# A four-stage expert pipeline, four buffers for normed rows, and logits read ahead of the maxima

## The chip, the cores and the metric

One core of one Trainium2 chip runs the whole kernel in one launch. The metric is the device time in microseconds, the median of several runs; before the change it is 1592.26 us.

## What is computed

Input: 16 sequences of 256 tokens with 256 features, float32. Two layers; in each, the attention part and the expert part both read the same normed rows, and both are added to the residual:

```
xn = layernorm(x)
x  = x + mamba(xn) + moe(xn; 8 experts, top 2, inner 512) + shared_ffn(xn; inner 512)
xn = layernorm(x)
x  = x + causal_attention(xn; 16 heads of 16) + moe(xn; 8 experts, top 2, inner 128) + shared_ffn(xn; inner 256)
```

The router takes a softmax over 8 logits per token, keeps the two largest and divides them by their sum. An expert computes silu(x Wg) * (x Wu) Wd.

## The kernel before

Sequences are the unit of the dense stages, tiles of 128 tokens of one expert the unit of the expert stages. Every engine has its own instruction list, all loops around the change are unrolled in Python, and the order in which a list holds the stages of different sequences or tiles is written out by hand; engines meet only at semaphores (`wait` and `mark` of an `Event`; the `credit` of an event is how far its producer may run ahead of its consumer).

The stages in order of time:

1. **Front of layer 0**, 0 to about 227 us (`first_turns`, line 130). For each of 16 sequences VectorE computes mean and variance, GpSimd the inverse root (L648), VectorE the normed rows (`norm_apply`, L1036, writing `XN`, L1042), SyncE stores them to `xn_rows` (L554), TensorE transposes them (L1600), ScalarE copies the transposes out (L812, L814), TensorE computes logits, VectorE reads them, picks two experts and computes each token's place in its expert's list, and GpSimd scatters token numbers into the lists (L657). The shared feed-forward runs between these on TensorE, ScalarE and VectorE. `XN` has two buffers. SyncE's queue also carries the loads of `x`, of the expert weights (8 loads of 1 MB into `WGU`, L556) and behind the last store those of `ARENA` (L558).
2. **Experts of layer 0**, 227 to 622 us, 71 tiles (`tile_turns`, L145; `experts` on three engines). GpSimd gathers a tile's rows (`gather_tile`, L703, L707) into a ring of four.
3. **Mamba**, 622 to 840 us.
4. **Attention of layer 1**, 840 to 1310 us: 16 turns of about 27 us (`attention` on each engine: L963 TensorE, L972 ScalarE, L1485 VectorE, L747 GpSimd). In one turn TensorE works on sequence b's scores, on d's weighted sums, on o's projection, and for the next sequence a on transposes, logits, queries and keys. VectorE computes the maxima of each group of heads (`maxima`, L1453) and shifts the queries by them (`shift`, L1461). PSUM bank 4 holds a's transposes, then its logits and rank sums, then its queries; so `queries(a, 0)` (L1877) waits until VectorE has copied the logits (`lgc`, L1057) and, for every second a, has read the rank sums (`rkc`, L1102).
5. **Experts of layer 1**, 1310 to 1514 us, 2 x 39 tiles (`last_turns`, L150), small: eight matmul records for gate and up together, two for the transpose, two for down. Eight of the 16 sequences of the shared feed-forward (`UPS`, L37; `EARLY`, L38) are laid between tile turns, and from tile 47 on (`FINALS_AT`) GpSimd issues one gather of the final sum (`fetch_final`, L767, L772) behind each tile's gather.
6. **The end**, 1514 to 1593 us: the other eight sequences of the feed-forward, the second half of the final gathers (which wait until the last tile is stored), the final sums on VectorE (`finish`, L1549) and the stores.

A turn of an expert stage, per engine, with tile j its middle stage:

```
TensorE   gate(j)  [up(j)]  xt(j+1)  down(j-1)
ScalarE   silu(j)  xt_copy(j+1)  y_copy(j-1)
VectorE   weights(j+1)  h(j)
```

`gate(j)` (L1799) needs `xt_copy(j)` (L903), which waits for the two transposes of `xt(j)` (L1793) of the turn before.

In VectorE's attention turn the order was: `maxima(b,2,0)`, `shift(b,0)`, `maxima(b,2,1)`, then `logits_stage(a)` and `place_tokens` (L1094: rank sums, then eleven small operations that make slots). TensorE's order is: rank sums, logits of a, `scores(1, now(2), now(0))`, `queries(a,0)`, `keys(a,0)`, `scores(0, now(3), now(0))`.

Of the kernel before, what the change touches and what calls it, by code (L numbers as in the profile page):

```python
# [18 lines left out]
P = 128  # L19
NSEQ, SEQ, D = 16, 256, 256  # L20
# [15 lines left out]
N1 = 2 * NH  # L36
UPS = {20: 0, 40: 1, 46: 2, 52: 3, 58: 4, 64: 5, 70: 6, 76: 7}  # L37
EARLY = len(UPS)  # L38
# [106 lines left out]
def tile_turns(count):  # L145

    return [[tile(t - k, count) for k in range(3)] for t in range(count + 2)]


def last_turns():  # L150


    end = N1 + 2
    for t in range(end + NSEQ - EARLY + 2):
        up = UPS.get(t) if t < end else EARLY + t - end
        down = UPS.get(t - 1) if t < end else EARLY + t - end - 1 if t > end else None
        last = (t - FINALS_AT - 3) // 4 if t < end and (t - FINALS_AT - 3) % 4 == 0 else EARLY + t - end - 2 if t > end + 1 else None
        yield t, [tile(t - k) for k in range(3)], *(None if n is None else of(n) for n in (up, down, last))

# [18 lines left out]
def program(nc, ctx, a, out):  # L178
# [82 lines left out]

    XN = [sb(f"XN{u}", [P, CH, D]) for u in range(2)]
    xT = [sb(f"xT{u}", [P, KD, SEQ]) for u in range(2)]
    stats = sb("stats", [P, CH, 6])
# [114 lines left out]
    def norm_events(l):  # L379
        b = l * NSEQ  # L380
        n = {name: ev(f"norm_{name}", credit, 1, eng, b) for name, credit, eng in (
            ("var", 0, None), ("rstd", 0, None), ("xn", 0, None), ("tr", 2, "tensor"), ("xT", 2, "scalar"),
            ("lg", 2, "tensor"), ("lgc", 2, "vector"))}
        n["stored"] = [ev(f"norm_stored{u}", 1, 16, "sync", b // 2) for u in range(2)]
        n["chain"] = Chain(norm_chain, 2, b)
        return n
# [135 lines left out]
    def _(eng):  # L522
# [27 lines left out]
        for n in range(NSEQ):  # L550
            if n + 6 < NSEQ:
                load_x(n + 6)
            N[0]["xn"].wait(eng, n)
            N[0]["stored"][n % 2].mark(eng.dma_start(rows0[:, n * CH:(n + 1) * CH, :], XN[n % 2][:, :, :]))  # L554
            if 3 <= n < 3 + E:
                eng.dma_start(wgu0[:, n - 3, :, :], a["gu0"][n - 3].rearrange("(k p) n -> p k n", p=P)).then_inc(s_wgu0, 16)  # L556
        for e in range(E):
            eng.dma_start(wdn0[:, e, :, :], a["dn0"][e].rearrange("(c p) n -> p c n", p=P)).then_inc(s_wdn0, 16)  # L558

# [48 lines left out]
    def _(eng):  # L608
# [101 lines left out]
        eng.wait_ge(s_slots, 1)  # L710
        for u in range(2):
            N[0]["stored"][u].wait(eng, NSEQ // 2 - 1)
        for j in range(NJ):
# [89 lines left out]
    def _(eng):  # L803
# [94 lines left out]
        def experts(l):  # L898
            x = EX[l]

            def xt_copy(r):
                x["xt"].wait(eng, r.n)
                x["xtc"].mark(act(XGT[r.u], bank[4][:, 0:KD * P].rearrange("p (k t) -> p k t", k=KD), ACT.Copy))  # L903

            def silu(r):
                x["g"].wait(eng, r.n)
                x["h"].wait(eng, r.n, 1)
                w = I0 if l == 0 else I1
                x["sg"].mark(act(SE[:, 0:w], bank[r.u][:, 0:w], ACT.Silu))  # L909

            def y_copy(r):
                x["dn"].wait(eng, r.n)
                x["out"][r.v].wait(eng, r.i, 1)
                x["yo"].mark(act(YO[r.v], bank[6 + r.u][:, 0:D], ACT.Copy))

            def body(new, r, old):
                if r:
                    silu(r)
                if new:
                    xt_copy(new)  # L920
                if old:
                    y_copy(old)
            return body
# [94 lines left out]
    def _(eng):  # L1018
# [17 lines left out]
        def norm_apply(l, r):  # L1036
            ne = N[l]
            ne["rstd"].wait(eng, r.n)
            ne["stored"][r.u].wait(eng, r.half, 1)
            ne["tr"].wait(eng, r.n, 2)  # L1040
            for c in range(CH):
                ins = ts(XN[r.u][:, c, :], X[:, bass.ds(r.n * CH + c, 1), :].rearrange("p a d -> p (a d)"),  # L1042
                         mv[r.u][:, c, 0:1], rstd[r.u][:, c:c + 1], ALU.subtract, ALU.mult)
            ne["xn"].mark(ins)
            ne["xn"].wait(eng, r.n)
# [47 lines left out]

        def place_tokens(l, m):  # L1094

            RT[l]["rank"].wait(eng, m)
            tiles = bass.ds(m * TB, TB)
            ranks = route_bank[l][:, RANK_AT:RANK_AT + (TB + 1) * E].rearrange("p (t e) -> p t e", e=E)
            ch = RT[l]["schain"]
            ch.start(eng, m)  # L1100
            ch(tt(at, ranks[:, 0:TB, :], run_e.unsqueeze(1).broadcast_to([P, TB, E]), ALU.add))
            RT[l]["rkc"].mark(tt(run_e, run_e, ranks[:, TB, :], ALU.add))  # L1102
            tt(pick[:, 0, :, :], at, OH[0][:, tiles, :], ALU.mult)
            ch(tt(pick[:, 1, :, :], at, OH[1][:, tiles, :], ALU.mult))
# [8 lines left out]
            ch.end()  # L1113
            RT[l]["slot"].mark(tt(slot_l[:, :, tiles], line, tile, ALU.bitwise_or))

        table_count = [0]
# [108 lines left out]
        def experts(l):  # L1225
# [32 lines left out]

            def body(new, r, old):
                if new and l == 1:  # L1260
                    both_weights(new)
                if new and l == 0 and new.n:
                    gate_weights(new)
                if r:
                    h_stage(r)
                if new and l == 0 and new.n:
                    up_weights(new)

# [216 lines left out]
        def attention(c, a, b, d, o):  # L1485
# [22 lines left out]
            if b:  # L1508
                maxima(b, 2, 0)
                shift(b, 0)  # L1510
                maxima(b, 2, 1)
            if a:
                logits_stage(1, a)
                if a.v == 0 and not is_first(a):
                    place_tokens(1, a.i - 1)
                if a.n == NSEQ // 2:
                    table_index(1)
                    next_lists()
                if a.n == 13:
                    list_done(1)  # L1520
                if a.v == 1:
                    pick_experts(1, a.i, [0])
# [63 lines left out]
    def _(eng):  # L1586
# [6 lines left out]
        def norm_stage(l, r):  # L1593
            ne = N[l]
            ne["xn"].wait(eng, r.n)
            ne["xT"].wait(eng, r.n, 1)
            b = bank[5 if l == 0 else 4]
            for c in range(CH):
                for k in range(KD):
                    ins = eng.transpose(b[:, k * SEQ + c * P:k * SEQ + (c + 1) * P],  # L1600
                                        XN[r.u][:, c, k * P:(k + 1) * P], ident[:, :])
            ne["tr"].mark(ins)
# [183 lines left out]
        def experts(l):  # L1786
# [38 lines left out]

            def body(new, r, old):
                if r:
                    gate(r)
                    if l == 0:
                        up(r)  # L1830
                if new:
                    xt(new)
                if old:
                    down(old)
            return body
# [241 lines left out]
```

## Time and profile before

| | |
|---|---|
| median of 3 runs | 1592.26 us (1591.78 to 1592.51) |
| profiled execution | 1595.26 us, its span 1593.5 us |
| mean granted TensorE clock | 0.954 |
| busy, share of the span | PE 91%, weight load 72%, VectorE 53%, ScalarE 33%, GpSimd 36% |
| matmul records | 10753 |
| moved by DMA | 94.77 MB, mean 59 GB/s |

Start times in rows are microseconds from the span's start. PE is TensorE, PEld its weight loads, DVE VectorE, ACT ScalarE, POOL GpSimd. L1591 is the helper through which nearly all matmuls are issued, so groups are told apart by their tiles: `score` is banks 0 to 3, `side` banks 4 and 5, `mixed` banks 6 and 7. The profile names an allocation and not a view of it: `ARENA`, `WGU`, `sh_gu` and `w_in` stand for whatever lies in them at the time (`WGU<-score` L1458 are the maxima).

### The profile page before, as it was taken

What the parts mean: (1) busy time and instruction counts of PE and PEld (TensorE: products, weight loads), DVE (VectorE), ACT (ScalarE), POOL (GpSimd) and SP (SyncE); (2) the same over time, 40 slices, a digit from 0 to 9 for tenths busy, and PEclk for the clock granted to TensorE, in tenths of its full rate; (3) what the DMA queues carried; (4) which work ended last, traced back from release to release, by engine and by line L of the source; (5) the groups of instructions that cost most, each with busy time, mean ns of one, the idle gap of its engine ahead of it and who ended that gap; (6) DMA issues with size and microseconds to landing.
All of it is one profiled execution on the core that took longest, in us unless ns stands there. A gap on an engine that the chain in (4) does not pass through costs nothing.

```text
span 1593.5 us, 29535 instructions
## 1 busy us (share of the span) xinstructions
PE 1453.8 (91%) x10753; PEld 1151.7 (72%) x10753; DVE 839.1 (53%) x2307; ACT 526.5 (33%) x1099; POOL 578.4 (36%) x762
## 2 busy tenths in 40 slices
PE   7996999999999998999997899999998979997866
PEld 6886789999999997666665566666665647776744
DVE  4554444444444443788875666666666534333414
ACT  2221122222222222333332545454444434433300
POOL 2444421111111111222224455646563454455460
PEclk9998999999999999999997999999999989999987
DMA  5893811111111114100002111111100004434431
GB/s 177 149 104 44 99 48 50 52 47 48 48 50 51 47 48 122 38 0 0 0 0 64 31 31 32 28 34 27 36 21 15 2 18 129 134 119 133 120 123 62
DMA packets 73185, 94.77 MB, mean 59 GB/s; under 512 B 14877, under 2 KB 61367, under 8 KB 73056
## 3 DMA queue, kind: packets, MB, share of 16 engines
q1 hardware_dynamic: 55440, 56.54, 15.6%
q0 software_dynamic: 17616, 36.48, 8.3%
q8 instruction: 84, 1.38, 0.4%
q14 instruction: 45, 0.37, 0.1%
HBM read 60.66 MB, written 32.31 MB: 58 GB/s over the span
## 4 chain that ended last, share of the span: by engine, by line
PE 86%; DVE 5%; issue 4%; DMA 2%; ACT 1%; another core or an unknown queue 1%; POOL 0%; DVEq 0%; ACTq 0%; POOLq 0%
PE score L1591 49%; PE mixed L1591 18%; PE side L1591 13%; DVE WGU L1458 2%; PE side L1793 2%; DMA xn_rows<-XN 2%; PE side L1600 1%; PE mixed L1960 1%; PE side L1953 1%; PE side L1739 0%; PE side L1858 0%; DVE stats L1027 0%; DVE X L1483 0%; DVE X L1558 0%
## 5 line engine op out<-in xcount | busy, mean ns | idle before, releaser
L707 POOL DMA_INDIRECT XN<-xn_rows,slot_tok x149 | 141.4, 949 | 399.5 <-PE side L1793 365.3
L1458 DVE TENSOR_REDUCE WGU<-score 128x2 f32<-128x256 f32 (+1 forms) x256 | 130.8, 553 | 153.3 <-PE score L1591 151.2
L1591 PE MATMUL score<-xT,HT 128*128 128x128 f32 x1136 | 208.0, 275 | 0.0
L743 POOL TENSOR_SCALAR_AFFINE_SELECT ARENA<-ARENA 128x256 f32<-128x256 f32 x256 | 104.2, 431 | 185.1 <-ACT ARENA L944 184.0
L1591 PEld LDWEIGHTS score<-xT,HT 128*128 128x128 f32 x1136 | 166.8, 192 | 0.0
L944 ACT ACTIVATE ARENA<-score 128x768 f32<-128x768 f32 x128 | 103.8, 811 | 148.3 <-PE score L1591 145.9
L1257 DVE TENSOR_TENSOR HT<-sh_gu,score 128x128 f32<-128x128 f32 (+1 forms) x149 | 71.3, 478 | 148.7 <-ACT sh_gu L909 71.3
L657 POOL DMA_INDIRECT lists<-token_no,w_in x128 | 125.4, 980 | 44.2 <-issue 32.3
L1591 PE MATMUL score<-ARENA 32*128 32x256 f32 (+1 forms) x2048 | 126.8, 353 | 12.0 <-DVE WGU L1458 6.0
L1591 PE MATMUL mixed<-ARENA,HT 128*128 x568 | 134.2, 379 | 0.0
L909 ACT ACTIVATE sh_gu<-score 128x128 f32<-128x128 f32 (+1 forms) x149 | 64.1, 430 | 191.3 <-PE score L1591 172.8
L1591 PE MATMUL score<-XT,sh_gu 128*128 128x256 f32 x512 | 120.3, 395 | 2.7 <-issue 2.7
L1232 DVE COPY xT<-WGU 128x256 f32 x142 | 35.5, 291 | 156.7 <-PE score L1591 155.9
L1591 PEld LDWEIGHTS score<-XT,sh_gu 128*128 128x128 f32 x512 | 101.2, 200 | 17.7 <-issue 3.3
L1591 PE MATMUL score<-xT 128*128 128x128 f32 x568 | 109.8, 275 | 2.4 <-issue 2.0
L1591 PEld LDWEIGHTS mixed<-ARENA,HT 128*128 128x128 f32 x568 | 102.5, 190 | 11.0
L1591 PEld LDWEIGHTS score<-xT,WGU 128*128 128x128 f32 x624 | 77.3, 193 | 45.6 <-ACT xT L903 35.2
L1591 PE MATMUL score<-xT,sh_gu 128*128 128x128 f32 x568 | 109.8, 275 | 0.0
L1591 PEld LDWEIGHTS score<-ARENA 32*128 32x128 f32 x2048 | 73.2, 188 | 50.3 <-issue 45.0
L1591 PE MATMUL side<-xT,WGU 128*128 128x256 f32 x256 | 88.6, 496 | 21.4 <-DVE w_in L1102 11.1
L1591 PE MATMUL score<-xT,WGU 128*128 128x128 f32 x624 | 89.7, 287 | 20.0 <-ACT xT L903 13.8
L1202 DVE TENSOR_TENSOR HT<-SG,score 128x256 f32<-128x256 f32 x96 | 39.7, 419 | 113.2 <-ACT SG L822 88.2
(249 smaller groups left out, 2714.8 us busy)
## 6 DMA issues: line engine op xcount, KB each, us to landing
y_rows<-sh_gu SPq DMA_DIRECT2D x149, 128.0 KB
xn_rows<-XN SPq DMA_DIRECT2D x32, 256.0 KB
WGU<-in_gu SPq DMA_DIRECT2D x8, 1024.0 KB
X<-in_u SPq DMA_DIRECT2D x16, 256.0 KB
ARENA<-in_dn SPq DMA_DIRECT2D x8, 512.0 KB
out<-X SPq DMA_DIRECT2D x16, 256.0 KB
XN<-xn_rows,slot_tok POOLq DMA_INDIRECT x149
lists<-token_no,w_in POOLq DMA_INDIRECT x128
```

The costliest lines, as they stand in the source:

```text
L657: eng.indirect_dma_start(lists, bass.IndirectOffsetOnAxis(slot_l[:, k, t:t + 1], 0), tok_i[:, t:t + 1], None).then_inc(s_scat[g], 16)
L707: x["got"][j % RING].mark(eng.indirect_dma_start(XG[j % RING], None, xn_rows[l], bass.IndirectOffsetOnAxis(slot_tok[:, j:j + 1], 0)))
L743: ins = eng.affine_select(out=m, in_=m, compare_op=ALU.is_ge, fill=0.0, base=0, pattern=[[0, 2], [1, P]], channel_multiplier=-1)
L909: x["sg"].mark(act(SE[:, 0:w], bank[r.u][:, 0:w], ACT.Silu))
L944: A["exp"][h].mark(act(PT[i % 2][:, 2 * h:2 * h + 2, :, :].rearrange("p r b q -> p r (b q)"), score[:, 2 * h:2 * h + 2, 0:HALVES * P], ACT ...
L1202: f["ht"].mark(tt(inner_rows(l, r, i), SG[i % 2][:, :], inner(l, r, i)[:, SEQ:2 * SEQ], ALU.mult))
L1232: ins = eng.tensor_copy(to, wgu0[:, bass.ds(expert(r), 1), k, first * P:end * P].rearrange("p a (c n) -> p (a c) n", n=P))
L1257: x["h"].mark(tt(HET[r.u][:, 0:w // P, :], parts(SE[:, 0:w]), parts(up), ALU.mult))
L1458: ins = eng.tensor_reduce(o, score[:, 2 * h:2 * h + 2, c * P:(2 * c + 1) * P], AX.X, ALU.max, negate=True)
L1591: return eng.matmul(o, l, r, start=start, stop=stop)
L1600: ins = eng.transpose(b[:, k * SEQ + c * P:k * SEQ + (c + 1) * P], XN[r.u][:, c, k * P:(k + 1) * P], ident[:, :])
L1793: ins = eng.transpose(bank[4][:, k * P:(k + 1) * P], XG[r.v][:, k * P:(k + 1) * P], ident[:, :])
```

## The change

The edits:

- **Expert turns have four stages**, in both layers: `xt` and `xt_copy` work on tile j+2 while gate works on j, and on TensorE `down` goes ahead of `xt`, on ScalarE `y_copy` ahead of `xt_copy`. VectorE's weights stay one tile ahead of gate. Each stage has one more turn.
- **Seven sequences of the feed-forward** instead of eight are laid between the tiles of layer 1, from the third on seven turns apart instead of six; nine are left for the end. The final sums move by two turns.
- **Four buffers for `XN` in the front of layer 0**: the two new ones lie in the part of `ARENA` that the last expert's down weights fill later; SyncE waits before that one load until both are stored and transposed.
- **VectorE's attention turn**: `logits_stage` and the rank sums stand between `shift(b,0)` and `maxima(b,2,1)`; the slots are made behind it. The copy of the turned list (a = 13) moves along with the logits.

```diff
-UPS = {20: 0, 40: 1, 46: 2, 52: 3, 58: 4, 64: 5, 70: 6, 76: 7}
+UPS = {20: 0, 40: 1, 46: 2, 53: 3, 60: 4, 67: 5, 74: 6}
...
-    return [[tile(t - k, count) for k in range(3)] for t in range(count + 2)]
+    return [[tile(t - k, count) for k in range(4)] for t in range(count + 3)]
...
-    end = N1 + 2
+    end = N1 + 3
+    finals = {FINALS_AT + 5 + 4 * n: n for n in range(EARLY)}
...
-        last = (t - FINALS_AT - 3) // 4 if t < end and (t - FINALS_AT - 3) % 4 == 0 else EARLY + t - end - 2 if t > end + 1 else None
-        yield t, [tile(t - k) for k in range(3)], *(None if n is None else of(n) for n in (up, down, last))
+        last = finals.get(t) if t < end else EARLY + t - end - 2 if t > end + 1 else None
+        yield t, [tile(t - k) for k in range(4)], *(None if n is None else of(n) for n in (up, down, last))
...
+    last_dn = ARENA[:, (E - 1) * I0 // P * D:].rearrange("p (u c d) -> p u c d", u=2, c=CH)
+    XN0 = [t[:, :, :] for t in XN] + [last_dn[:, u, :, :] for u in range(2)]
...
         for e in range(E):
+            if e == E - 1:
+                N[0]["tr"].wait(eng, NSEQ - 1)
+                for v in (2, 3):
+                    N[0]["stored"][v].wait(eng, NSEQ // len(XN0) - 1)
...
-            def body(new, r, old):
+            def body(new, ahead, r, old):
                 if r:
                     silu(r)
+                if old:
+                    y_copy(old)
                 if new:
                     xt_copy(new)
-                if old:
-                    y_copy(old)
...
             ne["rstd"].wait(eng, r.n)
-            ne["stored"][r.u].wait(eng, r.half, 1)
+            if l == 0:
+                rows, turn = XN0[r.n % len(XN0)], r.n // len(XN0)
+                ne["stored"][r.n % len(XN0)].wait(eng, turn, 1)
+            else:
+                rows = XN[r.u]
+                ne["stored"][r.u].wait(eng, r.half, 1)
...
                 shift(b, 0)
-                maxima(b, 2, 1)
             if a:
                 logits_stage(1, a)
                 if a.v == 0 and not is_first(a):
-                    place_tokens(1, a.i - 1)
+                    rank_sums(1, a.i - 1)
+                if a.n == 13:
+                    list_done(1)
+            if b:
+                maxima(b, 2, 1)
+            if a:
+                if a.v == 0 and not is_first(a):
+                    place_slots(1, a.i - 1)
                 if a.n == NSEQ // 2:
                     table_index(1)
                     next_lists()
-                if a.n == 13:
-                    list_done(1)
...
                 if r:
                     gate(r)
                     if l == 0:
                         up(r)
+                if old:
+                    down(old)
                 if new:
                     xt(new)
-                if old:
-                    down(old)
```

The hunks behind the list of `XN0` are, in this order, of SyncE's queue, ScalarE's expert turn, `norm_apply`, VectorE's attention turn and TensorE's expert turn. `rank_sums` and `place_slots` are the two halves of the old `place_tokens`, operation for operation.

## Rows read from the trace of the kernel before

**Rows 1.** The page, part 4: engines' shares of the chain that ended last
```profile
PE 86%; DVE 5%; issue 4%; DMA 2%; ACT 1%; another core or an unknown queue 1%; POOL 0%; DVEq 0%; ACTq 0%; POOLq 0%
```

**Rows 2.** Busy time by stretch: us of each engine, clock, DMA, GB/s
```profile
1400.00:1500.00 100.00, 84.55 (x504) 70.94 (x503) 37.35 (x102) 33.00 (x104) 59.40 (x63) 0.97 0.44 134
...
1540.00:1594.00 54.00, 27.97 (x98) 21.40 (x98) 21.86 (x49) 3.72 (x10) 13.49 (x15) 0.69 0.24 76
```

**Rows 3.** PE's timeline, 119 to 140 us (start, us, instruction, idle before)
```profile
122.19 0.66 PE L1600 MATMUL side<-ident,XN 128*128 128x128 f32 x4 [0.86 <-issue]
...
138.07 1.12 PE L1600 MATMUL side<-ident,XN 128*128 128x128 f32 x4 [10.98 <-DVE XN L1042]
```

**Rows 4.** VectorE's and GpSimd's timelines of the same stretch
```profile
121.39 0.74 DVE L1042 TENSOR_SCALAR XN<-X,mv,rstd 128x256 f32<-128x256 f32 x2 [3.23 <-issue]
...
137.28 0.74 DVE L1042 TENSOR_SCALAR XN<-X,mv,rstd 128x256 f32<-128x256 f32 x2 [9.00 <-DMA xn_rows<-XN]
...
128.37 0.72 POOL L648 TENSOR_TENSOR rstd<-rstd,minus_half 128x2 f32<-128x2 f32 x1 [4.71 <-DVE rstd L1034]
```

**Rows 5.** The waits, 860 to 1290 us (total us, times, longest)
```profile
PE side L1591 <- DVE w_in L1102: 11.1, 7, 1.6
...
PE side L1591 <- DVE LG L1057: 8.6, 7, 1.3
```

**Rows 6.** The chain that ended last, 860 to 1290 us (start, us, what)
```profile
872.36 3.78 PE side L1591 x8
...
898.91 1.97 PE side L1591 x8
...
1053.36 1.73 PE side L1591 x8
```

**Rows 7.** Busy time about one such wait, columns as in Rows 2
```profile
1006.00:1009.00 3.00, 1.99 (x5) 1.66 (x6) 2.45 (x14) 0.18 (x1) 1.73 (x3) 0.61 0.12 33
```

**Rows 8.** VectorE's timeline, 1055 to 1067 us, and a row of PE's
```profile
1057.36 0.86 DVE L1466 SCALAR_TENSOR_TENSOR ARENA<-side,head_mask,ARENA 128x256 f32<-128x256 f32 x2
1060.15 1.02 DVE L1458 TENSOR_REDUCE WGU<-score 128x2 f32<-128x256 f32 x2 [1.93 <-PE score L1591]
...
1066.04 0.17 DVE L1128 COPY w_in<-w_in 128x8 f32<-128x8 f32 x1
...
1057.88 1.04 PE L1591 MATMUL side<-WGU,xT 128*128 128x8 f32 x8
```

**Rows 9.** The waits, 1300 to 1520 us, and the chain, 1363 to 1399 us
```profile
PEld score L1591 <- ACT xT L903: 35.2, 50, 3.1
...
1363.66 1.16 PE score L1591 x8
...
1365.51 1.16 PE score L1591 x8
...
1391.43 4.34 PE score L1591 x24
...
1396.43 2.62 PE score L1591 x16
```

**Rows 10.** Costliest groups, 1402 to 1516 us (times, busy us, mean ns, idle before)
```profile
L772 POOL DMA_INDIRECT ARENA<-y_rows,slot x32 | 30.7, 959 | 9.7 <-issue 9.7
L707 POOL DMA_INDIRECT XN<-xn_rows,slot_tok x31 | 29.9, 964 | 31.2 <-PE side L1793 15.2 <-remote 10.8 <-issue 5.2
```

**Rows 11.** GpSimd's timeline at the end
```profile
1517.82 0.94 POOL L772 DMA_INDIRECT ARENA<-y_rows,slot  x1 [15.86 <-DMA y_rows<-sh_gu]
...
1556.81 0.95 POOL L772 DMA_INDIRECT ARENA<-y_rows,slot  x1 [0.30 <-issue]
```

**Rows 12.** The chain, 1515 to 1564 us
```profile
1528.51 3.45 PE score L1591 x16
...
1534.95 0.38 PE score L1591
...
1562.37 0.77 PE score L1591
```

More of the change, by code:

```diff
@@ L383, in norm_events @@
             ("lg", 2, "tensor"), ("lgc", 2, "vector"))}
-        n["stored"] = [ev(f"norm_stored{u}", 1, 16, "sync", b // 2) for u in range(2)]
+        n["stored"] = [ev(f"norm_stored{u}", 1, 16, "sync", b // len(XN0)) for u in range(len(XN0) if l == 0 else 2)]
         n["chain"] = Chain(norm_chain, 2, b)
@@ L553, in _ @@
             N[0]["xn"].wait(eng, n)
-            N[0]["stored"][n % 2].mark(eng.dma_start(rows0[:, n * CH:(n + 1) * CH, :], XN[n % 2][:, :, :]))
+            v = n % len(XN0)
+            N[0]["stored"][v].mark(eng.dma_start(rows0[:, n * CH:(n + 1) * CH, :], XN0[v]))
             if 3 <= n < 3 + E:
@@ L710, in _ @@
         eng.wait_ge(s_slots, 1)
-        for u in range(2):
-            N[0]["stored"][u].wait(eng, NSEQ // 2 - 1)
+        for v in range(len(XN0)):
+            N[0]["stored"][v].wait(eng, NSEQ // len(XN0) - 1)
         for j in range(NJ):
@@ L1038, in norm_apply @@
             ne["rstd"].wait(eng, r.n)
-            ne["stored"][r.u].wait(eng, r.half, 1)
+            if l == 0:
[4 more added lines that the diff above has]
+                ne["stored"][r.u].wait(eng, r.half, 1)
             ne["tr"].wait(eng, r.n, 2)
             for c in range(CH):
-                ins = ts(XN[r.u][:, c, :], X[:, bass.ds(r.n * CH + c, 1), :].rearrange("p a d -> p (a d)"),
+                ins = ts(rows[:, c, :], X[:, bass.ds(r.n * CH + c, 1), :].rearrange("p a d -> p (a d)"),
                          mv[r.u][:, c, 0:1], rstd[r.u][:, c:c + 1], ALU.subtract, ALU.mult)
@@ L1092, in pick_experts, with rank_sums @@
             RT[l]["hot"].mark(tt(hot_b[:, tiles, :], OH[0][:, tiles, :], OH[1][:, tiles, :], ALU.add))
-        def place_tokens(l, m):
+        def rank_sums(l, m):
             RT[l]["rank"].wait(eng, m)
-            tiles = bass.ds(m * TB, TB)
             ranks = route_bank[l][:, RANK_AT:RANK_AT + (TB + 1) * E].rearrange("p (t e) -> p t e", e=E)
@@ L1102, in place_tokens, with place_slots @@
             RT[l]["rkc"].mark(tt(run_e, run_e, ranks[:, TB, :], ALU.add))
+        def place_slots(l, m):
+            tiles = bass.ds(m * TB, TB)
+            ch = RT[l]["schain"]
             tt(pick[:, 0, :, :], at, OH[0][:, tiles, :], ALU.mult)
@@ L1114, in place_tokens @@
             RT[l]["slot"].mark(tt(slot_l[:, :, tiles], line, tile, ALU.bitwise_or))
+        def place_tokens(l, m):
+            rank_sums(l, m)
+            place_slots(l, m)
         table_count = [0]
@@ L1257, in h_stage, with body @@
                 x["h"].mark(tt(HET[r.u][:, 0:w // P, :], parts(SE[:, 0:w]), parts(up), ALU.mult))
[L1259 to L1263, printed above, removed]
+            def body(new, ahead, r, old):
+                if ahead and l == 1:
+                    both_weights(ahead)
+                if ahead and l == 0 and ahead.n:
+                    gate_weights(ahead)
                 if r:
                     h_stage(r)
-                if new and l == 0 and new.n:
-                    up_weights(new)
+                if ahead and l == 0 and ahead.n:
+                    up_weights(ahead)
             def first():
@@ L1597, in norm_stage @@
             b = bank[5 if l == 0 else 4]
+            rows = XN0[r.n % len(XN0)] if l == 0 else XN[r.u]
             for c in range(CH):
@@ L1600, in norm_stage @@
                     ins = eng.transpose(b[:, k * SEQ + c * P:k * SEQ + (c + 1) * P],
-                                        XN[r.u][:, c, k * P:(k + 1) * P], ident[:, :])
+                                        rows[:, c, k * P:(k + 1) * P], ident[:, :])
             ne["tr"].mark(ins)
@@ L1824, in down, with body @@
                 x["dn"].mark(ins)
-            def body(new, r, old):
+            def body(new, ahead, r, old):
                 if r:
```

## The prediction

> **What bounds the kernel now.** I read the chain that ended last first, then busy time by stretch, then the waits of each stretch, and only at disputed places the timelines. TensorE holds 86% of the chain [rows 1]; what it waits for, or does slowly, is the time to be had. A stretch where it is always busy gives nothing, so I looked for stretches where it is not: 84.55 of 100 us in the late tiles of layer 1, 27.97 of 54 us at the end at a granted clock of 0.69 [rows 2]. The experts of layer 0 are packed, and there I expect nothing but about +0.5 us for the extra turns.
>
> **1. Four buffers for normed rows.** The transposes at 138.07 waited 10.98 us for the normed rows [rows 3]; VectorE had begun them at 137.28 after 9.00 us of waiting for a store to leave `XN` [rows 4]. What is late next is the inverse root: it ends at 128.37+0.72=129.09, so with a free buffer the rows (0.74 us) are there at 129.83 and the transposes start near 130.0 instead of 138.07, 8.1 us sooner. The wait of 0.86 us at 122.19 [rows 3] belongs to the same pair of buffers (VectorE's rows began at 121.39 [rows 4]). Sum **-8.9**. The store that a buffer needs next is four sequences back, over 20 us earlier, and 9 us were the most that one was late. SyncE's queue gets one new wait, ahead of the last down weights only; behind it stand loads for experts 100 us later, so I cost it at nothing; uncovered it would be one late load of that kind, up to 9 us. Bounds -6 (a later sequence takes 3 us back) and -11.
>
> **2. Logits ahead of the maxima.** Between 860 and 1290 us TensorE waits 11.1 us for the rank sums and 8.6 us for the logits' copy, 7 times each [rows 5]. VectorE starts the second half's maxima only when the scores end, idle 1.93 us before; the logits (1.04 us from 1057.88) end at 1058.92 and the shift (0.86 from 1057.36) at 1058.22 [rows 8]. So copy and sums, some 0.5 us, fit into that idle time, before 1060.15, and both waits go: **-19.7**. Maxima, if late, have cover: TensorE comes to their buffer behind queries and keys, 1.73 us at full clock, against 1.02 for the maxima [rows 8], 0.7 us. Its bounds are -15 (0.35 us a turn left) and -19.7.
>
> **3. The clock behind those waits.** Queries and keys are eight records: 3.78 us at 872.36, 1.97 at 898.91 [rows 6]. Of the 15 such rows of the turns 13 take 3.43 to 3.78 us, 3.57 on average, which is half speed (1.2 of 2.4 GHz); about one of the waits the granted clock is 0.61 [rows 7]. Eight records of another stage, with work ahead of them, take 1.73 at 1053.36 [rows 6], 0.216 each. A wait stands in front of every slow row but the first, at 872.36, so I let the clock go with the wait: twelve turns from 3.57 to 1.97, and in the fourteen turns with waits 0.24 us from 1.97 to 1.73: 19.2+3.4=**-22.6**. Bounds 0 and -22.6. One rule speaks against this. The Trainium skill, "TensorE: Matmul & The Clock Gate", Part 4 on PE-mode transpose, says that transposes don't count as activity the way matmuls do. Attention has transposes in every turn, which the change leaves there; by that rule the clock would stay low without any wait, and this term would be nothing.
>
> In the turn a=8 the table is now built ahead of the other maxima of the next group: it holds VectorE to 1066.04 [rows 8], where these are due 3 us behind the last. 2.4 us of wait and 1.7 us of slow records: **+4.1**, bounds 0 and +5.
>
> **4. Tile turns of layer 1.** One turn is 1365.51-1363.66=1.85 us [rows 9], four parts in a chain: gate 1.16, transposes, down, and a wait for ScalarE's copy: 35.2 us over 50 waits of the weight load on `xT` [rows 9]. Gate costs 1.16 because its first load waits; where eight feed-forward records stand ahead of it the sixteen take 2.62 [rows 9], of which 8 x 0.216=1.73 (the side records, [rows 6]) are theirs, and gate has 0.89. Transposes and down take 1396.43-(1391.43+4.34)=0.66. With the copy a whole turn old, a turn is 0.89+0.66=1.55, 0.31 less. About 40 turns stand before the final gathers start: **-12**. The nearest floor is GpSimd's issue: 0.96 us busy [rows 10], and in the final burst (1556.81-1517.82)/31=1.26 from one to the next [rows 11], under 1.55. Bounds 0 and -15.
>
> **5. The late tiles.** From 1402 to 1516 us GpSimd issues 32 final gathers and 31 tile gathers, 30.7 and 29.9 us busy; before the latter it is idle 31.2 us, put down to TensorE's transposes and to an unknown releaser [rows 10]. TensorE is idle there too [rows 2], so neither is plainly the bound. One feed-forward sequence leaves this stretch (its 5.18 us comes back in 6), but GpSimd's two issues per tile, 2.5 us, may then hold the tiles. Between the two I take **-4**: nearest to the row that says GpSimd still waits for TensorE for 15.2 us. Bounds +10 (GpSimd holds all tiles) and -20 (idle time of TensorE gone).
>
> **6. The end.** Nine sequences stand behind the tiles, not eight: 3.45+1.73 us [rows 12, 6], **+5.2**. But from 1534.12 to 1562.37 the chain has a record only every (1562.37-1534.95)/13=2.1 us [rows 12], while GpSimd issues final gathers back to back from 1517.82 to 1557.8 [rows 11]: TensorE seems held by that burst. The sequence more is dearer if it falls into it. Bounds +5.2 and +30.
>
> **Sum:** 0.5-8.9-19.7-22.6+4.1-12-4+5.2=-57.4. The profiled execution has 1595.26 us (span 1593.5) and would come to 1537.9; the median of the runs, 1592.26, is 3.0 lower: **1535**.
>
> **The rivals.** A measurement of this kernel can tell about 0.2% (3.2 us) from no change.
>
> - *The tile turns give nothing* (0.14): the ring of four fills at GpSimd's pace, since gathers are issued when `XG` is freed by a transpose, and terms 4 and 5 fall away, +16. For it: GpSimd's idle time is partly "issue" [rows 10]. Against: PE's load waits for ScalarE, 35.2 us, not for a gather. **1551**.
> - *The clock stays low in attention* (0.09): something else in the turn than the wait lowers it. For: the two turns at 1.97 don't show why they are spared. Against: the rows of a turn that have work ahead of them are at full clock [rows 6]. Term 3 gives nothing, +22.6: **1558**. That is what the page's rule on transposes would make of it; the front speaks against it, where four transposes take 0.66 us behind a wait of 0.86 and 1.12 behind one of 10.98 [rows 3], so that they follow the wait.
> - *The tail's held stretch goes* (0.08): with TensorE further behind or ahead of the burst, the 13 records between 1534.95 and 1562.37 take 0.216 instead of 2.1 us each, 13 x 1.9=-24: **1511**.
> - *VectorE is late in the shorter attention turns* (0.05): with turns some 3 us shorter the eleven slot operations and maxima compete, 0.7 us in each of 14 turns: +10, **1545**.
> - *Slower: TensorE is held while GpSimd issues back to back* (0.04). The mechanism of the tail, in two places: with the copy a turn early GpSimd no longer waits for transposes in the late tiles [rows 10] and issues back to back there too. Each record so held costs 2.1-0.2=1.9 us. The whole extra sequence of the tail (24 records) and as many in the late tiles are 48 x 1.9=91: 1535+91=**1626**. It decides from 57/1.9=30 held records on. Against: the late tiles have fewer records beside the burst after the change, and GpSimd's waits there have TensorE as releaser.
> - *No effect* (0.02): the waits come back under other names, as when VectorE's order is right but each turn is set by ScalarE: **1592**.
>
> The forecast has 0.58.
>
> **How the numbers follow.** 1535 is the likeliest case. Its own bounds lie in terms 3 to 6; 1508 holds the case of the freed tail and nearly all of -20 in term 5, 1562 holds the cases at 1545, 1551 and 1558 with what can go wrong in one of them besides. What is left out is the slower rival, no effect, and mixtures of two large misses. Within 0.2%: 0.02, from "no effect"; slower: 0.04, from the last mechanism; faster: the rest, 0.94.
>
> **What would show each step.** (1) TensorE's wait at 127 to 138 us shrinks from 10.98 to about 3; the wait for `xn_rows` leaves VectorE's list. (2) Both groups of waits of [rows 5] vanish, the attention turn falls by (19.7+22.6)/14=3.0 us. (3) All rows of queries and keys stand at 1.73 to 1.97 us; at 3.5 with the waits gone, the clock rival is right. The turn a=8 alone shows a wait for `WGU`. (4) The weight load's wait for `xT` is gone and early turns are 1.55 us apart; at 1.85, the first rival holds, and what TensorE waits for (`XT`, an unknown releaser) says whose pace it is. (5) The stretch from the first final gather to the last tile is 4 us shorter with nine feed-forward sequences behind; GpSimd without idle time there and TensorE with more would prove me wrong. (6) Nine sequences at the end, each 5.18 us outside the burst; records 2 us apart over more than one sequence point to the slower mechanism. The forecast as a whole is wrong if attention does not end at least 35 us sooner relative to its start.

## The result, and the profile after

The changed kernel takes 1543.97 us (median of 4 runs, 1535.74 to 1551.84) beside 1592.12 us before (4 runs): a ratio of 0.9697, 95% interval 0.9633 to 0.9761, so 48 us or 3.0% less. The forecast was 1535 us with a range of 1508 to 1562: the measured time lies in the range, 9 us above the forecast. The profiled execution is the fastest of the four: 1535.74 us, its span 1533.2 us, 60.3 us shorter than the span of before. The table cuts both spans at the same instructions of GpSimd. That is the first thing to do with two traces: where a stage comes out equal, nothing was won or lost in sum (though two effects can still cancel in it).

| stretch | before | after | difference |
|---|---|---|---|
| start to the first gather of layer 0 | 221.5 | 211.6 | -9.9 |
| to the first gather of layer 1 | 1079.6 | 1036.3 | -43.3 |
| to the first early final gather (the early tiles) | 101.5 | 91.4 | -10.1 |
| to the first final gather of the burst (the late tiles) | 115.2 | 114.4 | -0.8 |
| to the last one | 39.0 | 39.0 | 0.0 |
| to the end (the rest of the span) | 36.7 | 40.5 | +3.8 |

The burst is what GpSimd does behind the last tile: it issues the last 32 final gathers one after the other.

**Front.** TensorE's timeline of the changed kernel answers [rows 3]: the wait of 10.98 us is 1.93, and the next group of transposes stands at 127.23 instead of 138.07.

```profile
127.23 0.76 PE L1626 MATMUL side<-ident,XN 128*128 128x128 f32 x4 [1.93 <-DVE XN L1055]
...
137.37 0.63 PE L1626 MATMUL side<-ident,ARENA 128*128 128x128 f32 x4
```

**Attention.** Both groups of [rows 5] are gone from TensorE's waits; the longest entries left are those for maxima and shift, which were there before with 6.0 and 4.4 us. Columns: total us, times, longest.

```profile
PE score L1616 <- DVE WGU L1479: 7.9, 8, 2.7
PE score L1616 <- DVE ARENA L1487: 4.9, 5, 1.9
```

The chain shows queries and keys at full clock, where [rows 6] had 3.78, and beside them the exception, the first turn (859.15). (Columns: start, us, what.)

```profile
859.15 2.96 PE side L1616 x8
...
1004.32 1.73 PE side L1616 x8
...
1056.63 1.73 PE side L1616 x8
```

The granted clock of the stretch about the second of them, the column before the DMA share, is 1.00 in the busy time by stretch, against 0.61 in [rows 7].

```profile
1003.00:1006.00 3.00, 3.00 (x32) 2.15 (x31) 1.66 (x6) 1.59 (x3) 1.63 (x3) 1.00 0.23 56
```

**Tiles.** In a typical early turn the chain has no wait left: from one gate to the next 1315.28-1313.73=1.55 us, against 1.85 in [rows 9].

```profile
1313.73 0.89 PE score L1616 x8
1314.62 0.43 PE mixed L1616 x2
1315.06 0.22 PE side L1819 x2
1315.28 0.89 PE score L1616 x8
```

Not every turn is like that. In three turns, of 2.2 to 2.4 us, VectorE has operations on the tables of tiles, slots and weights in front of the copy of an expert's weights (L1266), and gate starts only 0.1 us after that copy ends. One of them:

```profile
1279.97 0.48 DVE L1196 TENSOR_REDUCE route_small<-SG 128x16 f32<-128x128 f32 x2
...
1280.66 0.42 DVE L1266 COPY WGU<-WGU 128x512 f32 x1
...
1281.18 1.13 PE L1616 MATMUL score<-xT,WGU 128*128 128x128 f32 x8 [0.50 <-issue]
```

**The late tiles and the end.** The late tiles took as long as before with one feed-forward sequence less in them. GpSimd's two groups are those of [rows 10] almost number for number; what differs is its idle time ahead of the tile gathers, 27.2 us instead of 31.2, with 10.6 instead of 15.2 us put down to TensorE's transposes. The part without a known releaser ("remote") stayed, 10.5 beside 10.8.

```profile
L780 POOL DMA_INDIRECT ARENA<-y_rows,slot x32 | 31.2, 976 | 9.7 <-issue 9.7
L715 POOL DMA_INDIRECT XN<-xn_rows,slot_tok x31 | 29.8, 962 | 27.2 <-PE side L1819 10.6 <-remote 10.5 <-issue 5.5
```

In the timeline GpSimd issues transfers with 0.3 us between them. ScalarE waits 3.93 us, until 1384.28, for the gate whose eight records stand at 1379.12 to 1380.25, and TensorE starts again when GpSimd has paused:

```profile
1378.17 0.97 POOL L715 DMA_INDIRECT XN<-xn_rows,slot_tok  x1 [0.30 <-issue]
...
1379.12 1.13 PE L1616 MATMUL score<-xT,WGU 128*128 128x128 f32 x8 [0.64 <-issue]
...
1379.44 0.95 POOL L780 DMA_INDIRECT ARENA<-y_rows,slot  x1 [0.30 <-issue]
...
1380.70 0.95 POOL L715 DMA_INDIRECT XN<-xn_rows,slot_tok  x1 [0.31 <-issue]
...
1381.95 0.95 POOL L780 DMA_INDIRECT ARENA<-y_rows,slot  x1 [0.30 <-issue]
...
1384.28 0.28 ACT L917 ACTIVATE sh_gu<-score 128x128 f32<-128x128 f32 x1 [3.93 <-remote]
...
1385.03 0.69 PE L1616 MATMUL mixed<-WGU,HT 128*128 x2 [3.22 <-DVE HT L1278]
```

At the end GpSimd issues 32 final gathers from 1453.74 to 1493.6, and from 1470.8 on TensorE has one record in 0.7 to 3.5 us, with nothing to wait for ("issue"), until 1498.9. That is the held stretch of [rows 12], about as long as before.

```profile
1453.74 0.94 POOL L780 DMA_INDIRECT ARENA<-y_rows,slot  x1 [18.24 <-DMA y_rows<-sh_gu]
...
1480.67 0.58 PE L1616 MATMUL score<-XT,WGU 128*128 128x256 f32 x1 [1.52 <-issue]
...
1483.45 0.58 PE L1616 MATMUL score<-XT,WGU 128*128 128x256 f32 x1 [2.20 <-issue]
...
1492.69 0.95 POOL L780 DMA_INDIRECT ARENA<-y_rows,slot  x1 [0.30 <-issue]
...
1493.96 0.59 PE L1616 MATMUL score<-XT,WGU 128*128 128x256 f32 x1 [2.91 <-issue]
```

TensorE's own rows don't show all of it. Outside such stretches ScalarE's silu of the feed-forward starts 0.42 us after the start of the last of the eight records that it needs. In the burst the silu at 1466.56 comes 4.2 us after its record (1462.32), and the two of the group at 1464.26, with last records at 1465.78 and 1467.50, come 26.1 and 31.4 us after them. VectorE's sum at 1472.94 comes 8.5 us after the end of its eight records, which begin at 1462.54.

```profile
1462.54 1.89 PE L1616 MATMUL side<-WGU,HT 128*128 128x256 f32 x8
1464.26 3.62 PE L1616 MATMUL score<-XT,WGU 128*128 128x256 f32 x16
1466.56 0.38 ACT L830 ACTIVATE SG<-score 128x256 f32<-128x256 f32 x1 [5.17 <-PE score L1616]
...
1472.94 0.69 DVE L1228 TENSOR_TENSOR X<-X,side 128x512 f32<-128x512 f32 x1 [5.54 <-remote]
...
1491.87 0.38 ACT L830 ACTIVATE SG<-score 128x256 f32<-128x256 f32 x1 [24.93 <-remote]
...
1498.89 0.66 ACT L830 ACTIVATE SG<-score 128x256 f32<-128x256 f32 x2 [6.64 <-remote]
```

So by what the other engines get from TensorE the hold begins some 9 us into the burst (1462.3 against 1453.74), earlier than TensorE's gaps say. The ends of matmul records are modelled, so the trace doesn't tell whether TensorE finished late or the others were held as well. "TensorE is held" stands below for this whole effect.

### The profile page after: what moved, and what is told of

The parts are those of the page before. It is cut to its first block, busy times and chain, and to the rows that moved or that the text cites. A ratio compares the mean times of both kernels' runs of the same rounds, so it can differ in the third digit from the quotient of the medians.

```text
span 1533.2 us, 29539 instructions
## 1 busy us (share of the span) xinstructions
PE 1420.3 (93%) x10753; PEld 1139.0 (74%) x10753; DVE 826.0 (54%) x2307; ACT 516.3 (34%) x1099; POOL 579.7 (38%) x762
## 4 chain that ended last, share of the span: by engine, by line
PE 87%; DVE 4%; another core or an unknown queue 3%; issue 3%; ACT 1%; POOL 1%; DVEq 0%; POOLq 0%; ACTq 0%
PE score L1616 49%; PE mixed L1616 20%; PE side L1616 13%; PE side L1819 2%; PE side L1626 1%; DVE WGU L1479 1%; PE mixed L1986 1%; PE side L1979 1%; PE side L1765 1%; DVE stats L1035 0%; PE side L1884 0%; POOL lists L665 0%; DVE X L1583 0%; DVE ARENA L1390 0%
## 5 line engine op out<-in xcount | busy, mean ns | idle before, releaser
L922 ACT ACTIVATE sh_gu<-mixed 128x256 f32<-128x256 f32 x149 | 57.1, 383 | 224.6 <-PE mixed L1616 216.9
L830 ACT ACTIVATE SG<-score 128x256 f32<-128x256 f32 x96 | 36.3, 383 | 185.6 <-PE score L1616 128.8
L1616 PE MATMUL score<-xT,WGU 128*128 128x128 f32 x624 | 86.0, 282 | 5.8 <-ACT xT L911 3.6
```

The costliest lines, as they stand in the source:

```text
L830: f["sg"].mark(act(SG[i % 2][:, :], inner(l, r, i)[:, 0:SEQ], ACT.Silu))
L1616: return eng.matmul(o, l, r, start=start, stop=stop)
```

## The experiments

Each kernel was timed beside the kernel before on the same chip. Those chips differ (before had medians of 1595, 1590 and 1603 us in the three groups of runs, against 1592), and the runs of one kernel with four or more of them spread by 4 to 20 us there, so ratios count. Each cut of code shows the main lines of an edit and leaves the rest out. Group one: each edit by itself, and the changed kernel with eight sequences between the tiles.

**Four buffers alone.** Its edit, on the kernel before:

```diff
+    XN0 = [t[:, :, :] for t in XN] + [last_dn[:, u, :, :] for u in range(2)]
...
-            N[0]["stored"][n % 2].mark(eng.dma_start(rows0[:, n * CH:(n + 1) * CH, :], XN[n % 2][:, :, :]))
+            v = n % len(XN0)
+            N[0]["stored"][v].mark(eng.dma_start(rows0[:, n * CH:(n + 1) * CH, :], XN0[v]))
```

> The kernel before with the four buffers for normed rows alone. My theory: the two waits of TensorE in the front go, the first gather of layer 0 comes 9 to 10 us sooner, and nothing later takes it back: 1583 us (-9). The rival (the gain is taken back where the last down weights now wait): the first experts of layer 0 wait for weights, 1592 us.

Measured: ratio 0.9972 (0.9951 to 0.9993), 4.5 us instead of 9. The waits did go: the last transposes of the front stand at 144.96 instead of 154.50. But the first gather came at 223.0, no sooner than before's 221.5. The 9.5 us were lost again between 153 and 193 us (the feed-forward's groups start 9.5 us sooner than before at 145.5 and 4.3 us later at 193.5). Part of it went in held stretches like those at the end; TensorE's idle time put down to "issue" in the rest of the front is 8.8 us against 3.4 in the kernel before: GpSimd issues eight scatters to the lists in a row, and TensorE's records, which wait for nothing, come 2 to 3 us apart.

```profile
143.54 0.96 POOL L664 DMA_INDIRECT lists<-token_no,w_in  x1 [4.18 <-DVE w_in L1126]
...
144.96 0.66 PE L1613 MATMUL side<-ident,ARENA 128*128 128x128 f32 x4 [1.27 <-DVE ARENA L1054]
...
152.37 0.96 POOL L664 DMA_INDIRECT lists<-token_no,w_in  x1 [0.30 <-issue]
...
153.54 0.17 PE L1603 MATMUL mixed<-w_r,xT 128*128 128x12 f32 x1 [0.88 <-issue]
156.34 0.17 PE L1603 MATMUL mixed<-w_r,xT 128*128 128x12 f32 x1 [2.63 <-issue]
158.44 1.25 PE L1603 MATMUL mixed<-w_r,xT 128*128 128x12 f32 x6 [1.93 <-issue]
```

The same buffers taken out of the changed kernel:

```diff
-            v = n % len(XN0)
-            N[0]["stored"][v].mark(eng.dma_start(rows0[:, n * CH:(n + 1) * CH, :], XN0[v]))
+            N[0]["stored"][n % 2].mark(eng.dma_start(rows0[:, n * CH:(n + 1) * CH, :], XN[n % 2][:, :, :]))
```

> The changed kernel without the four buffers for normed rows, so with two. My theory of the buffers (8.9 us of waits go and nothing takes them back): 7 to 10 us slower than the changed kernel, 1549 to 1552. The rival, as the run with the buffers alone suggests (part of the gain is lost to held stretches of TensorE later in the front, or the wait covered such a stretch): 3 to 6 us slower, and the two waits of 8 to 11 us for VectorE's normed rows are back.

Measured: ratio 0.9744 (0.9705 to 0.9782) against 0.9697, some 7 us slower, with intervals that overlap. TensorE's waits for normed rows are 28.1 us in 8 waits, against 15.1 and 16.3 us in the two traces of the changed kernel, so 12 to 13 us of waits are back:

```profile
PE side L1613 <- DVE XN L1043: 28.1, 8, 7.7
```

By the two runs the buffers are worth 4.5 to 7 us in the median, not 8.9.

**VectorE's order alone.**

```diff
                 shift(b, 0)
-                maxima(b, 2, 1)
             if a:
                 logits_stage(1, a)
...
+            if b:
+                maxima(b, 2, 1)
```

> The kernel before with VectorE's new order in attention alone. My theory: both groups of waits go, 19.7 us, and the clock with them, 22.6 us, so 1592 - 42 + 4 (the turn with the table) = 1554, at most 1550. The rival (the clock is low there for another reason than the wait): only the waits go, 1572 to 1576, and queries and keys still take 3.4 to 3.8 us.

Measured: ratio 0.9766 (0.9726 to 0.9805), 37 us less, 1556 us. That is the sum with the clock in it (38 us by the prediction's terms); the waits alone would have given 1572 to 1576. In its trace queries and keys take 1.73 us in nearly every turn and 3.27 in the first. The rival in which something else lowers the clock is out. (The chain, the first turn and a later one:)

```profile
871.64 3.27 PE side L1603 x8
...
1017.04 1.73 PE side L1603 x8
```

**Four-stage turns alone.**

```diff
-    return [[tile(t - k, count) for k in range(3)] for t in range(count + 2)]
+    return [[tile(t - k, count) for k in range(4)] for t in range(count + 3)]
...
-            def body(new, r, old):
+            def body(new, ahead, r, old):
```

> The kernel before with four-stage expert turns alone, eight feed-forward sequences still between the tiles. My theory: a turn without a sequence takes 1.55 us instead of 1.85 until the final gathers start, 40 x 0.31 = 12 us, and nothing or a little more in the late tiles: 1580 (1575 to 1585). The rival (TensorE is held while GpSimd issues back to back, and it now does so sooner): part of the 12 us comes back in the late tiles, 1586 to 1600.

Measured: ratio 0.9906 (0.9873 to 0.994), 15 us less, 1579.5 us; early tiles 91.8 us instead of 101.5, late tiles 112.3 instead of 115.2. Of what the late tiles could have given, 31 times 0.3 us, only a third came.

**Eight sequences between the tiles.**

```diff
-UPS = {20: 0, 40: 1, 46: 2, 53: 3, 60: 4, 67: 5, 74: 6}
+UPS = {20: 0, 40: 1, 46: 2, 52: 3, 58: 4, 64: 5, 70: 6, 76: 7}
```

> The changed kernel with eight feed-forward sequences between the tiles, six turns apart, as before the change. Theory A (the end is set by the last tile, GpSimd's 40 us of final gathers behind it, in which TensorE does three sequences and then is held, and the sequences left after that): the last tile is 5 us later and one sequence less is left, the same within 3 us. Theory B (my sum, where the ninth sequence costs 5.2 us at the end and frees less in the late tiles): 1 to 5 us faster than the changed kernel. If more sequences collide with pairs of gathers in the late tiles: 5 to 15 us slower.

Measured: ratio 0.966 (0.9597 to 0.9724), beside 0.9697: no difference that these runs can tell; if there is one, the move to seven sequences cost a few us. In its trace the late tiles take 109.0 us with one sequence more in them than the changed kernel's 114.4, and the end behind the burst is 4.6 us shorter.

**What holds TensorE.** Six traces of group one and of before and after have the same end: the first wait of TensorE over 0.6 us comes 17 to 20 us after the burst's first gather, its first stage behind the held stretch starts 7.0 to 7.3 us after the last gather's start, whatever stood in between. So the held stretch moves with the burst. Group two gave GpSimd a pause (`pause(5)`: five fills of 128x128, each awaited, 1.3 us together; its definition isn't shown) or took the burst away.

```diff
         for q in range(NSEQ * CH, NSEQ * CH * TOPK):
+            if q % (CH * TOPK) == 0:
+                pause(5)
             fetch_final(q)
```

> The changed kernel with a pause of GpSimd of about 1.3 us ahead of every four of the 32 final gathers at the end. Theory A (TensorE is held, one instruction in 0.7 us or more, once GpSimd has issued indirect transfers back to back for some time): the held stretch at the end goes, the burst is 10 us longer, the end comes 10 to 20 us sooner. Theory B (TensorE is held by the gathers' traffic as such, or by their number): the held stretch stays and lasts as long as the burst, so the end comes 8 to 12 us later.

Measured: 1519.16 us (1510.79 to 1528.84), ratio 0.9539 (0.9467 to 0.9611), against 1541.95 us for the changed kernel on the same chip: 23 us faster, more than the 10 to 20 expected, with all 32 gathers still there. The burst is 49.8 us long instead of 39, and TensorE isn't held at all: every silu in it comes 0.42 us after its record. TensorE is busy 43.10 of 52 us there, against 23.60 of 46. Columns of the two windows, here of this kernel: length, busy us of PE, PEld, DVE, ACT, POOL, clock, DMA share, GB/s. The core's DMA moves 119 GB/s here and 99 there, so the sum of its traffic isn't what holds TensorE.

```profile
1469.00:1521.00 52.00, 43.10 (x200) 37.61 (x198) 26.24 (x58) 6.50 (x17) 38.53 (x68) 0.97 0.39 119
```

The same of the changed kernel:

```profile
1453.00:1499.00 46.00, 23.60 (x93) 17.92 (x92) 5.79 (x13) 2.40 (x7) 30.46 (x32) 0.75 0.33 99
```

The surplus is stores of results, which are late in the changed kernel. The gathers' own queue moved 4.07 MB in the 52 us and 4.20 MB in the 46, 78 and 91 GB/s: with pauses they are spread out a little, and no run tells the pauses from the lower pace of the gathers. (Columns: packets, MB, share.)

```profile
q0 software_dynamic: 1488, 4.07, 27.0%
```

```profile
q0 software_dynamic: 1536, 4.20, 30.8%
```

GpSimd's timeline with pauses shows one between two groups of four:

```profile
1469.73 0.95 POOL L790 DMA_INDIRECT ARENA<-y_rows,slot  x1 [0.50 <-POOL rest L665]
...
1473.49 0.94 POOL L790 DMA_INDIRECT ARENA<-y_rows,slot  x1 [0.30 <-issue]
1474.43 1.28 POOL L665 MEMSET rest<- 128x128 f32 x5
1476.21 0.95 POOL L790 DMA_INDIRECT ARENA<-y_rows,slot  x1 [0.51 <-POOL rest L665]
```

The chain now ends with the last gather's landing, so GpSimd is the bound there and no longer TensorE:

```profile
1519.53 2.79 DMA ARENA<-y_rows,slot
```

For comparison the changed kernel itself:

> The changed kernel once more, for comparison with the others on the same chip and for its spread: 1535 to 1552.

Measured: 1541.95 us (1540.23 to 1544.43), ratio 0.9701 (0.9636 to 0.9767).

And without the burst. This kernel leaves the last 32 final gathers out, so its results are wrong and only its time counts; the wait for them goes too.

```diff
-        for q in range(NSEQ * CH, NSEQ * CH * TOPK):
-            fetch_final(q)
```

> The changed kernel without the 32 final gathers behind the last tile (the final sums of sequences 8 to 15 then use whatever lies in the buffers). Both theories: no held stretch, TensorE does its nine sequences in 9 x 5.18 = 47 us, and the kernel ends 25 to 30 us sooner, near 1510. If a held stretch of records 1.4 to 2.1 us apart still shows there, GpSimd's issues are not its cause.

Measured: 1518.23 us (2 runs), 24 us less than the changed kernel beside it, where I had 25 to 30, and no held stretch at the end. The pauses get as much as leaving the gathers out.

**The front with pauses.**

```diff
             if a and a.n > 2:
                 if a.n == 3:
                     eng.wait_ge(s_zero, 16)
+                pause(5)
```

> The changed kernel with a pause of about 1.3 us ahead of each group of four scatters to the lists in the front of layer 0. Theory A: the held stretches there (2 to 6 us each, at a different place in every run) go, the first gather of layer 0 comes at 210 us in each run, and the spread narrows: 0 to 8 us faster than the changed kernel. Theory B: no difference, or 1 to 2 us slower where GpSimd is late.

Measured: 1537.4 us (1533.12 to 1548.86), ratio 0.9692 (0.961 to 0.9775). The spread is not narrower, and the difference to the changed kernel isn't distinguishable. In its trace one held record is left in the front, 0.78 us, against three or four in the two traces of the changed kernel; that is one trace, and it settles nothing about the time.

**The late tiles.** Group three took the early final gathers out (the results are wrong then, and only the time counts), or put pauses there:

```diff
             if j >= FINALS_AT and done < NSEQ * CH:
-                fetch_final(done)
                 done += 1
```

> The changed kernel without the 32 final gathers between the late tiles (sequences 0 to 7 then use whatever lies in the buffers). If these gathers hold TensorE, tile turns stay at 1.55 us up to the last tile and the stretch of late tiles is 92 to 95 us instead of 114, ending near 1520; if tiles are set by something else, it stays above 105 us.

Measured: ratio 0.9523 (0.9473 to 0.9573), 1528.05 us where before has 1603.17. From the 48th gather of layer 1 to the last it is 70.6 us; the changed kernel has 94.0 (1338.08 to 1432.06).

```profile
1349.73 0.94 POOL L715 DMA_INDIRECT XN<-xn_rows,slot_tok  x1 [0.61 <-DMA y_rows<-sh_gu]
...
1420.34 0.94 POOL L715 DMA_INDIRECT XN<-xn_rows,slot_tok  x1 [0.85 <-issue]
```

Between these two gathers lie 30 tile turns: 30 at 1.55 and four sequences at 5.18 are 67.2 us, and three turns with longer waits make the rest. So TensorE is nearly packed there once the final gathers are gone, and these cost 23.4 us in the changed kernel. Up to the burst, the end of the stretch, it is 90.3 us without them and 115.7 with them.

The silus show a hold here too. In the changed kernel 14 of the late tiles' silus come 1.1 to 5.2 us after the last gate record that they need, together 38 us later than the usual 0.31; in the kernel before it is 11 silus and 20 us; without the final gathers none comes over 1 us after it. Pauses get a part of it:

```diff
             if j >= FINALS_AT and done < NSEQ * CH:
+                if done % 3 == 0:
+                    pause(5)
                 fetch_final(done)
```

> The changed kernel with a pause of GpSimd of about 1.3 us at every third late tile, 11 pauses in all. If TensorE is held there by issues back to back, as at the end, its 20 us of held idle time shrink and the kernel ends 3 to 12 us sooner, 1530 to 1539. If GpSimd's own pace sets the late tiles, each pause adds to it: up to 14 us slower.

Measured: ratio 0.9643 (0.9604 to 0.9683), against 0.9697 and 0.9701 for the changed kernel: about 9 us faster, but the intervals overlap and the changed kernel wasn't timed on this chip. From the 48th gather to the burst it is 110.0 us, against 115.7 and 117.0 in the two traces of the changed kernel, with 14 us of pauses in it: 6 to 7 us of the 25 that the gathers cost. Almost all of it lies behind the last tile's gather; up to that the stretch takes 93.7 us, against 94.0 and 96.6. The front of this trace was slow for another reason: even four buffers were full, and VectorE waited for a store 13.1 us:

```profile
DVE ARENA L1067 <- DMA xn_rows<-ARENA: 22.0, 2, 13.1
```

**All of it.** The last kernel puts these together: eight sequences, the pauses in the front and in the late tiles, and one ahead of every eight gathers of the burst.

```diff
         for q in range(NSEQ * CH, NSEQ * CH * TOPK):
+            if q % (2 * CH * TOPK) == 0:
+                pause(5)
             fetch_final(q)
```

> All that helped so far in one kernel: the changed kernel with eight sequences between the tiles, a pause ahead of each group of four scatters in the front, one at every third late tile, and one ahead of every eight of the last 32 gathers. With groups of eight, 10 us of issues, below the 17 to 20 us behind which TensorE was held at the end, the burst is 45 us and the held stretch stays away: 1505 to 1515. If eight in a row already hold TensorE, it is 1515 to 1525.

Measured: ratio 0.9451 (0.9415 to 0.9487), 1514.77 us (1508.49 to 1523.14) where before has 1603.17 on the same chip. It beats both kernels, the one before by 5.5% and the changed one by 2.5%, by the ratios. The absolute times don't compare with my 1505 to 1515 from a faster chip; 0.9451 of 1592.12 would be 1505. The burst is 43.7 us, and the long hold is gone. A short one is left: from 1476 us on the burst's silus come 1.5 to 3.7 us after their records, where with groups of four it is 0.42. So eight in a row, 10 us of issues, already hold the engines for a moment, as eight scatters do in the front. Against the kernel with pauses in the burst alone (0.9467 to 0.9611) the intervals overlap.

## Why the prediction was right, step by step

- **Four buffers, -8.9.** The profiled execution has -9.9 up to the first gather. The median has 4.5 to 7. What was too large is the silent assumption that the rest of the front passes the whole gain on; the prediction had 3 us taken back only as a bound. The kernel before has two such held records at 193.5 and 194.9 us, and the prediction didn't count them. The other step, that no store is over 9 us late with four buffers, failed in one trace (13.1 us). Held stretches lie at a different place in each trace, and a wait for a buffer and a held stretch partly cover each other. The transposes came at 127.2 and not at 130.0, where I had put them by the inverse root of before; why the whole sequence ran 3 us sooner wasn't traced.
- **Logits ahead of the maxima, -19.7, and the clock, -22.6.** Right in mechanism, and a little too small. Typical turns went from 27.33 us to 24.1 (transposes of successive turns at 971.77, 995.87, 1019.91), 3.2 us where I had 3.0. The whole stretch to the first gather of layer 1 lost 43.3 us, where its terms (0.5, -19.7, -22.6, +4.1) add up to -37.7: 36.8 between the first and the last transposes of attention, 4.5 behind them and 2.0 ahead of them. Only the first turn is above 1.92 us for queries and keys. The transposes stand in every turn as before and the clock is 1.00, so the rule of the Trainium skill ("TensorE: Matmul & The Clock Gate", Part 4, PE-mode transpose), that they don't count as activity, decides nothing here.
- **The turn with the table, +4.1.** Right: transposes 1019.91 to 1048.19, 28.3 us, 4.2 above its neighbours, and the longest wait for maxima is 2.7 us, where I had 2.4.
- **Tile turns, -12.** The turn is 1.55 us as forecast, and the count of 40 was right too: between the transposes of the first and the 44th tile lie 39 turns without a sequence, and the kernel before takes 1.85 us for 35 of them. What the sum left out is VectorE. Seven turns of the changed kernel take 1.9 to 2.4 us, and in three of them gate waits for the copy of an expert's weights behind operations on the tables. The longer turn had hidden that almost: the slowest turn of the kernel before takes 1.97 us. These seven cost 4 us, and a quicker start gives 1 back: 12.1-3.0=9.1 us, and the first transposes come another 1.0 sooner after the first gather.
- **Late tiles, -4.** Measured -0.8. With 31 faster turns and one sequence less, 9+5 us were on offer and nearly all was given back. I had both numbers and no cause, and took a middle. The final gathers cost 25 us of this stretch, and the silus that come late (38 us in sum, 20 before) show that the hold grew. That it is the hold alone isn't shown: pauses won back 6 to 7 us only, and GpSimd's own pace, 2.5 us for two issues, is longer than a turn.
- **The end, +5.2.** Measured +3.8. The burst is pinned to the last tile's store, and TensorE's records in it don't depend on what is laid there; the sequence more was done behind it. The slower rival had the right mechanism, TensorE held while GpSimd issues back to back, and the wrong place: it priced records in the burst at 1.9 us each, while a longer list doesn't lengthen the stretch.

The sum was -57.4 and the profiled execution has -60.3. That they lie so close is in part luck: attention and what stands around it gave 5.6 us more than forecast, the tiles 5 us less. The median is 9 us above the forecast because the four runs lie 16 us apart and the profiled one is the fastest. Which part of a slower run is longer is seen in one pair of traces only: the second trace of the changed kernel, 1540.3 us, has the first gather 2.9 us later, the stretch to layer 1 is 1.6 us longer, the late tiles are 1.4 longer and the end 1.2.

## What to carry to other kernels

A wait that goes is worth more than its length where the clock falls behind it, but only the trace says so: compare the same eight records with and without a wait ahead. An engine that shows gaps put down to "issue", on the critical path and in many places, may have a cause outside its own list; look at how late the readers of its results start, and at what the other engines issue in those microseconds before laying more work there. Where GpSimd issues many indirect transfers in a row, a short pause between groups can be worth more than the pause costs; here it was at the end, and hardly in the front and the late tiles.

## What the runs showed that I had not expected

- Behind 8 to 10 us of GpSimd's scatters in the front, and behind 17 to 20 us of its gathers at the end, TensorE starts one instruction in 0.7, 1.4, 2.1 or more us though it waits for no semaphore, at 5.75 us busy in 27 (1472 to 1499). It goes on for some 5 us after the last issue. ScalarE and VectorE get TensorE's results late from some 9 us into the burst on, about as early as in the front. A pause of 1.3 us every four issues prevents it, with as many bytes moved; every eight issues, 10 us, it leaves delays of up to 3.7 us. What inside the chip hands this from one engine to the other is open: no run looked at it. A late load of instructions isn't seen: in the changed kernel the last packet of an instruction queue ahead of the stretch was over before 1466 us, none follows before 1499, and the gaps began at 1470.8.
- A pause helped, but idle time of GpSimd isn't free everywhere: in the late tiles pauses got 6 to 7 of 25 us, and more pauses or another distance weren't tried.
- The kernel before has medians of 1590 to 1603 us on the chips of this case, and the front of kernels with the same front differs by up to 26 us between traces (211.6 and 237.4), in the slower of which VectorE waited 22.0 us for stores of normed rows in spite of the four buffers.
